# Deformable convolution, attention and routed FFN on one core: a later far list, later far sums, offset rows ahead of the projections, residual copies moved on ScalarE

## The chip, the core and the metric

The kernel runs on one core of a Trainium2 chip. The metric is the device time of one execution in microseconds. The kernel before takes 690.18 us, the median of 3 runs (689.71 to 691.6).

## The reference

The input is `x`, 4 images of 32 x 32 positions and 128 channels, all float32. Three blocks follow one another, each added to its input:

1. A deformable convolution of the group-normed `x`. A depthwise 3x3 convolution, a batch norm and SiLU give `x1`; `x1 @ off_w` gives 2-D offsets and `softmax(x1 @ mask_w)` weights, for 8 groups of channels and 9 points each. The projected input `xp` is sampled bilinearly at the 9 points (position + offset), weighted and summed, and the sum goes through `out_w`:

```
out  = corner(x0, y0, (1-fx)*(1-fy)) + corner(x0+1, y0, fx*(1-fy))
     + corner(x0, y0+1, (1-fx)*fy)   + corner(x0+1, y0+1, fx*fy)
out  = (samples * mask).sum(points) @ out_w + out_b
```

2. Attention over the 1024 tokens of each image, with layer norm ahead of it.
3. A layer norm, two routed experts of eight for each image (GELU, 128 to 256 to 128), and a layer norm of their sum.

The change touches only the first block.

## The kernel before, in words

**Sampling without a gather.** Most sample positions lie near their own place. For each position the kernel builds a 7 x 7 stencil of weights per group from "hats" (the bilinear weights of an offset against five places on each axis), and multiplies the 45 used places ("taps", the four corners of the 7 x 7 are left out) with shifted copies of `xp`. Samples whose cells fall outside the stencil are "far": they are counted, listed, fetched by GpSimd one by one with indirect DMAs, and added as a correction.

**Chunks and turns.** The work is cut into 8 chunks of 4 image rows (`CHUNKS`), with all 4 images side by side: 512 positions, 128 partitions x 4 rows. The engines run a software pipeline. In turn k:

- VectorE (`turn`, `stencils`, `products`) multiplies the taps of chunk k (L1591, 26 instructions of one or two taps) and in between prepares the stencil of chunk k+1: `mask_logits` (row_max L1447), `masks`, `weigh_hats` (L1476), `corners`, and then nine points, each an outer product (L1524) and an add into the stencil (L1532). The two kinds are interleaved by `fill`: two product instructions behind each point's outer product, `POINT_FILL`, and two more after the last add, `STENCIL_FILL`. The far list of chunk k+1 is made by `list_far(k+1)`, one MAX8 (L1578) over the counts in PSUM, ahead of the point `AT_LIST` = 4 counted from 0, the fifth. `finish_silu` (L1437) stands ahead of the sixth point. `first_stencils` prepares chunk 0 and makes list 0 at the same point. The list goes to a buffer of its own, so `list_far` waits for `far_done` (the counts are copied out) and for `list_taken` (GpSimd has copied the list before).
- TensorE (`turn` L923 on) sums each tap into a PSUM bank by four 128x128 transposes (`add_up`, L890). It waits for the product of the tap and frees its slot. There are 7 product slots, one per column of the stencil, so a tap's product can be written only when the last tap of the same column is summed. Between the sums stand, by tap number: the convolution of chunk k+2 (`AT_CONV` = 4, nine taps, L834), the counts of far samples of chunk k+1 (`AT_FAR` = 18, `count_far`, L873 to L876), the correction of chunk k-1 from GpSimd (`AT_SAMPLES` = 24, `add_fix`, L897, which waits for `fix_done`), the projection of chunk k-1, one image at every second tap (`AT_PROJECT` = 27, `project`, L909 to L912, which waits for ScalarE's `copy_out`), and the offset matmuls of chunk k+2, one row at every second tap (`AT_OFFSETS` = 32, `offsets`, L826 and L827).
- ScalarE (`turn(j)` L659, j = k) copies the offsets of chunk j+2 out (`prepare`, L590), makes its hats (L602, L608), clears the stencil (L638), makes the signs for the counts (L617) and the SiLU parts (L576, L577), copies the counts out for GpSimd (`count_out`, L647, which waits for `fix_done` of iteration j), copies the samples of chunk j out (`copy_out`, L624), and copies the projected residual of chunk j (`residual`, L632, which waits for the projection in TensorE's turn j+1).
- GpSimd runs one iteration per chunk (L1315 on): copy the list (L1322), move the places (L1323), clear and signal `list_taken` (L1326, L1327), then for each listed sample: take its offsets (L1221 to L1223), its cells (L1230 to L1240), four indirect DMAs (L1244), the corner weights (L1252 to L1277), and multiply and add what came (L1284 to L1289). At the end it signals `fix_done` (L1345).
- SyncE's queue fetches the shifted copies for the later chunks when the products of a chunk are done.

After the eighth chunk, whose products stand alone, come the attention (from about 437 us) and the FFN.

Of the kernel before, what the change touches and what calls it, by code (L numbers as in the profile page):

```python
# [40 lines left out]
CHUNKS = H // ROWS  # L41
# [21 lines left out]
UNITS = len(UNIT_AT)  # L63

BEGIN = 2
AT_CONV, AT_FAR, AT_SAMPLES, AT_PROJECT, AT_OFFSETS = 4, 18, 24, 27, 32


AT_LIST = 4


AT_SILU = 5
# [73 lines left out]
def hybrid_block_kernel(nc, x, in_w, in_b, out_w, out_b, off_w, off_b, mask_w, mask_b, dw_k, bn_g, bn_b,  # L146
                        bn_m, bn_v, attn_w, wr, br, w1, b1, w2, b2, gamma, beta, out):
    padded = nc.dram_tensor("padded", (WP, B, HP, C), F32, kind="Internal").ap()
    with ExitStack() as ctx:
# [397 lines left out]
        def _(sc):  # L547
            own = Own(sc, act)
# [62 lines left out]
            def signs_of(k):  # L611
                raw = pair[0][:, :].rearrange("p (r o) -> p r o", r=ROWS)
                if not isinstance(k, int) or k > 0:
                    sc.wait_ge(far_mm, k)
                    sc.sem_inc(act_waited, 1)
                for i, sign in enumerate((1.0, -1.0)):
                    last = sc.activation(signs[:, i, :, :], raw[:, :, 0:2 * GP], ACT.Sign,  # L617
                                         bias=tap_bias[:, TAPS - 1:TAPS], scale=sign)
                last.then_inc(signs_done, 1)
# [7 lines left out]
            def residual(k):  # L627
                sc.wait_ge(conv_out, k + 1)
                sc.sem_inc(act_waited, 1)
                to = res[:, :, :].rearrange("p (n k) c -> p n k c", n=B)[:, :, bass.ds(k, 1), :] \  # L630
                    .rearrange("p n k c -> p n (k c)")
                sc.activation(to, bank[0][:, :].rearrange("p (n c) -> p n c", n=B), ACT.Copy).then_inc(res1_done, 1)  # L632

            def clear_stencil(k):

                sc.wait_ge(prod_done, (k + 1) * NEAR)
                sc.sem_inc(act_waited, 1)
                sc.activation(stencil[:, bass.ds(k % 2, 1), :].rearrange("p s g -> p (s g)"),  # L638
                              zero_col[:, 0:1].to_broadcast([P, ROWS * G * STENCIL]), ACT.Copy
                              ).then_inc(stencil_clear, 1)  # L640
# [18 lines left out]
            def turn(j, conv_ahead):  # L659
                prepare(j + 2)  # L660
                clear_stencil(j)
                signs_of(j + 2)
                if conv_ahead:
                    silu(j + 3)
                count_out(j + 2)
                copy_out(j)
                residual(j)

            with sc.Fori(0, CHUNKS - 3) as j:
                own.enter(j, TAPS)  # L670
                turn(j, True)
                own.leave(CHUNKS - 3)
            turn(CHUNKS - 3, False)

            def residual_of(k, n0, n1):
                at = k % 2
# [702 lines left out]
        def _(ve):  # L1379
            own = Own(ve, dve)  # L1380
# [128 lines left out]
            def stencils(k, fill, silu_next):  # L1509
# [6 lines left out]
                for q in range(PTS):  # L1516
                    kx, ky = q // 3, q % 3
                    to = now[:, :, ky:ky + TAPS, kx:kx + TAPS]
                    own.wait()
                    if q == AT_LIST:  # L1520
                        list_far(k)
# [14 lines left out]
            def first_stencils():  # L1536

                ve.wait_ge(stencil_clear, 1)
                hx = hats[:, 0, :, :].rearrange("p (g q) t -> p g q t", q=PTS)
                hy = hats[:, 1, :, :].rearrange("p (g q) t -> p g q t", q=PTS)  # L1540
                full = [P, ROWS * G, TAPS, TAPS]
                size = ROWS * G * TAPS * TAPS
                spare = prod[:, :, :, :].rearrange("p s g c -> p (s g c)")
                held = [outer[:, :, :, :]] + [spare[:, i * size:(i + 1) * size].rearrange("p (g a b) -> p g a b", a=TAPS, b=TAPS)
                                              for i in range(3)]

                def place_of_point(q):
                    ky, kx = q % 3, q // 3
                    return stencil_of[:, 0, :, ky:ky + TAPS, kx:kx + TAPS]

                def point_product(q):
                    own(ve.tensor_tensor(place_of_point(0) if q == 0 else held[q % 4],
                                         hy[:, :, q, :].unsqueeze(3).to_broadcast(full),
                                         hx[:, :, q, :].unsqueeze(2).to_broadcast(full), ALU.mult))

                own.wait()
                point_product(0)
                point_product(1)
                for q in range(1, PTS):
                    if q + 1 < PTS:  # L1560
                        point_product(q + 1)
                        ve.wait_ge(dve, own.base + own.n - 1)
                    else:
                        own.wait()
                        ve.sem_inc(hats_used, 1)  # L1565
                    if q == AT_LIST:
                        list_far(0)
                    if q == AT_SILU:
                        finish_silu(1)
                    own(ve.tensor_tensor(place_of_point(q), place_of_point(q), held[q % 4], ALU.add))  # L1570
                own.wait()
# [25 lines left out]

            ve.sem_inc(res1_done, 1)
            first_stencils()
            per = own.n - n0  # L1600
            products(0, 0, BEGIN)
# [255 lines left out]
```

## Time and profile before

| | us |
|---|---|
| median of 3 runs | 690.18 (689.71 to 691.6) |
| profiled execution | 690.75 |
| its span | 688.9 |
| TensorE / VectorE / ScalarE / GpSimd busy | 588.7 / 565.8 / 234.3 / 338.8 |
| mean granted TensorE clock | 0.937 |

Busy time by stage of the profiled execution:

| stretch (us) | length | TensorE | VectorE | ScalarE | GpSimd | granted clock |
|---|---|---|---|---|---|---|
| 0 to 65.14, set-up and chunk 0's stencil | 65.14 | 52.59 | 44.81 | 30.12 | 30.24 | 0.95 |
| 65.14 to 412, turns 0 to 6 | 346.86 | 278.92 | 330.47 | 101.42 | 253.50 | 0.90 |
| 412 to 437, products of chunk 7 | 25.00 | 23.50 | 24.63 | 1.20 | 0.73 | 1.00 |
| 437 to 688.9, attention and FFN | 251.90 | 233.67 | 165.90 | 101.58 | 54.36 | 0.98 |

A busy TensorE is not TensorE at its peak, since matmuls are pipelined. The granted clock is a share of 2.4 GHz: 1.00 is 2.4 GHz and 0.50 is 1.2 GHz. Times in a timeline are microseconds from the start of the span, and a merged row is followed by the number of its instructions (x4).

### The profile page before, as it was taken

What the parts mean: (1) busy time and instruction counts of PE and PEld (TensorE: products, weight loads), DVE (VectorE), ACT (ScalarE), POOL (GpSimd) and SP (SyncE); (2) the same over time, 40 slices, a digit from 0 to 9 for tenths busy, and PEclk for the clock granted to TensorE, in tenths of its full rate; (3) what the DMA queues carried; (4) which work ended last, traced back from release to release, by engine and by line L of the source; (5) the groups of instructions that cost most, each with busy time, mean ns of one, the idle gap of its engine ahead of it and who ended that gap; (6) DMA issues with size and microseconds to landing.
All of it is one profiled execution on the core that took longest, in us unless ns stands there. A gap on an engine that the chain in (4) does not pass through costs nothing.

```text
span 688.9 us, 11121 instructions
## 1 busy us (share of the span) xinstructions
PE 588.7 (85%) x3518; PEld 434.8 (63%) x3518; DVE 565.8 (82%) x1028; ACT 234.3 (34%) x343; POOL 338.8 (49%) x407
## 2 busy tenths in 40 slices
PE   5988879879779589599786779889999999989995
PEld 4556566556556366376565567567777777775774
DVE  4589999999999699699999999726776776654877
ACT  6164306206125016107125000334545444424431
POOL 7505885888588578658667940201222221124322
PEclk9899959999999699879988799999999999999998
DMA  7096303003003007000000000000000000004111
GB/s 189 33 342 222 118 0 108 3 3 108 1 2 109 0 2 270 0 1 3 0 1 5 0 1 1 1 0 1 1 1 1 1 0 1 1 1 119 44 39 46
DMA packets 26238, 30.71 MB, mean 45 GB/s; under 512 B 5572, under 2 KB 18324, under 8 KB 26196
## 3 DMA queue, kind: packets, MB, share of 16 engines
q1 hardware_dynamic: 24094, 29.77, 13.2%
q0 software_dynamic: 1408, 0.36, 0.6%
q8 instruction: 28, 0.46, 0.3%
q10 hardware_dynamic: 694, 0.01, 0.1%
q14 instruction: 14, 0.11, 0.1%
HBM read 25.07 MB, written 5.05 MB: 44 GB/s over the span
## 4 chain that ended last, share of the span: by engine, by line
PE 38%; POOL 15%; DVE 15%; DMA 14%; issue 11%; POOLq 3%; ACT 1%; DVEq 1%; SPq 0%; ACTq 0%
DMA got<-padded,cell_now 11%; PE banks L1009 8%; PE pair L989 8%; DVE prod L1591 7%; POOL got L1244 6%; PE pair L1067 4%; PE banks L999 4%; PE banks L890 4%; PE banks L1105 4%; POOL cell_now L1240 2%; DVE stencil L1532 2%; DMA padded<-stage 2%; PE pair L834 1%; POOL place L1323 1%; POOLq L1300 1%
## 5 line engine op out<-in xcount | busy, mean ns | idle before, releaser
L890 PE MATMUL banks<-ident,prod 128*128 128x128 f32 x1440 | 219.7, 295 | 63.5 <-DVE prod L1591 61.2
L890 PEld LDWEIGHTS banks<-ident,prod 128*128 128x128 f32 x1440 | 174.2, 150 | 125.2 <-DVE prod L1591 98.4
L1591 DVE TENSOR_TENSOR prod<-shifted,stencil 128x1024 f32 (+3 forms) x208 | 216.1, 1079 | 0.1
L1349 POOL TENSOR_TENSOR rstd_now<-mv_now,neg_half 128x2 f32<-128x2 f32 x32 | 23.0, 718 | 126.1 <-DVE mv_now L1642 126.1
L834 PE MATMUL pair<-xg,dw_diag 128*128 128x512 f32 x144 | 73.4, 611 | 0.7 <-DVE xg L1403 0.7
L1244 POOL DMA_INDIRECT got<-padded,cell_now x44 | 63.6, 1446 | 19.0 <-issue 10.1
L1009 PEld LDWEIGHTS banks<-shifted 128*128 128x128 f32 x512 | 60.2, 192 | 8.1 <-issue 6.1
L1009 PE MATMUL banks<-shifted 128*128 128x128 f32 x512 | 63.3, 277 | 2.3 <-ACT shifted L714 1.4
L989 PE MATMUL pair<-shifted 128*128 128x512 f32 x128 | 60.9, 598 | 0.7 <-ACT shifted L697 0.6
L1657 DVE TENSOR_REDUCE neg_max<-pair 128x1 f32<-128x1024 f32 x32 | 39.2, 1225 | 23.0 <-PE pair L989 21.9
L1524 DVE TENSOR_TENSOR outer<-hats 128x800 f32<-128x800 f32 x56 | 56.1, 1002 | 1.2
L1532 DVE TENSOR_TENSOR stencil<-stencil,outer 128x800 f32 (+1 forms) x56 | 55.8, 997 | 0.0
L602 ACT ACTIVATE hats<-off,tap_bias 128x576 f32 (+1 forms) x40 | 48.4, 1342 | 1.3 <-DVEq L1565 0.5
L709 ACT ACTIVATE shifted<-pair,neg_max 128x1024 f32<-128x1024 f32 x32 | 35.7, 1115 | 33.5 <-DVE neg_max L1657 33.5
L1662 DVE COPY shifted<-banks 128x512 f32<-128x512 f32 x32 | 22.1, 689 | 22.5 <-PE banks L999 22.5
L1355 POOL TENSOR_TENSOR res<-res,bias_all 128x256 f32 x16 | 11.6, 727 | 46.2 <-DVE xg L1648 46.2
L999 PE MATMUL banks<-ident,shifted 128*128 128x128 f32 x256 | 34.1, 277 | 0.0
L989 PEld LDWEIGHTS pair<-shifted 128*128 128x128 f32 x128 | 22.0, 192 | 16.9 <-issue 15.3
L999 PEld LDWEIGHTS banks<-ident,shifted 128*128 128x128 f32 x256 | 30.2, 144 | 1.3 <-issue 0.2
L1067 PE MATMUL pair<-shifted,stage 128*128 128x512 f32 x64 | 29.3, 597 | 1.5 <-DMA stage<-in_L_ffn_W_dram 1.5
L632 ACT ACTIVATE res<-banks 128x512 f32 (+1 forms) x6 | 3.6, 597 | 79.0 <-PE banks L912 79.0
L834 PEld LDWEIGHTS pair<-xg,dw_diag 128*128 128x128 f32 x144 | 23.9, 197 | 10.0 <-issue 10.0
(250 smaller groups left out, 918.8 us busy)
## 6 DMA issues: line engine op xcount, KB each, us to landing
shifted<-padded SPq DMA_DIRECT2D x42, 256.0 KB
shifted<-padded SPq DMA_DIRECT2D x14, 640.0 KB
res<-in_x_dram SPq DMA_DIRECT2D x4, 512.0 KB, 6.2
padded<-stage SPq DMA_DIRECT2D x4, 512.0 KB, 11.8
stage<-in_L_ffn_W_dram SPq DMA_DIRECT2D x16, 128.0 KB, 2.1
out_dram<-res SPq DMA_DIRECT2D x16, 128.0 KB, 1.8
got<-padded,cell_now POOLq DMA_INDIRECT x44
padded<-stencil SPq DMA_DIRECT2D x2, 228.0 KB, 2.6
```

The lines of the kernel that those rows point to most:

```text
L602: own(sc.activation(hats[:, :, :, t].rearrange("p a (r g) -> p a r g", r=ROWS), off[:, bass.ds(k % OFFS, 1), :, 0:2 * GP].rearrange("p s r ...
L834: mm = pe.matmul(conv_bank.rearrange("c (r a) -> c r a", r=ROWS), dw_diag[:, t, :], src, start=(t == 0), stop=(t == 8))
L890: mm = pe.matmul(acc_of(c, r), prod[:, slot, r * G:(r + 1) * G, :].rearrange("p g c -> p (g c)"), ident[:, :], is_transpose=True, start=(t ...
L989: mm = pe.matmul(pair[s][:, h * 512:(h + 1) * 512], keyed[:, bass.ds(i * P, P)], normed_t[:, bass.ds((i // TILES) * TOK + h * 512, 512)], ...
L999: mm = pe.transpose(bank[h][:, m * P:(m + 1) * P], probs[:, s, (4 * h + m) * P:(4 * h + m + 1) * P], ident[:, :])
L1009: mm = pe.matmul(bank[2][:, 0:C], probs_t[:, m * P:(m + 1) * P], normed[:, bass.ds((i // TILES) * TILES + m, 1), :].rearrange("p t c -> p ...
L1067: pe.matmul(pair[j][:, (f % 2) * 512:(f % 2 + 1) * 512], w1_sel[:, 2 * (q // 2) + j, (f % 2) * P:(f % 2 + 1) * P], normed2_t[:, q * 512:(q ...
L1244: gp.indirect_dma_start(out=got[:, j, a, :], out_offset=None, in_=table, in_offset=bass.IndirectOffsetOnAxis(ap=cell_now[:, j, a:a + 1], a ...
L1524: own(ve.tensor_tensor(to if q == 0 else outer[:, :, :, :], hy[:, :, q, :].unsqueeze(3).to_broadcast(full), hx[:, :, q, :].unsqueeze(2).to ...
L1532: own(ve.tensor_tensor(to, to, outer[:, :, :, :], ALU.add))
L1591: ins = ve.tensor_tensor(prod[:, dx:dx + n, :, :], shifted[:, dx:dx + n, bass.ds(((c % HALF) * ROWS + dy) * G, ROWS * G), :], stencil_of[: ...
L1657: ve.tensor_reduce(neg_max[:, s:s + 1], pair[s][:, :], AX.X, ALU.max, negate=True).then_inc(max_done, 1)
```

## The change

Five edits. The far list of chunks 1 to 7 is made ahead of the ninth stencil point, `AT_LIST` = 8; that of chunk 0 stays at the fifth, under the name `FIRST_LIST`. On TensorE the correction (`add_fix`) goes from tap 24 to tap 31, also in the last chunk, where `AT_SAMPLES` is used by itself. The projections go from taps 27, 29, 31, 33 to taps 35, 37, 39, 41. The offset rows go from taps 32, 34, 36, 38 to taps 30, 32, 34, 36, so that they stand ahead of the projections. On ScalarE `residual(j - 1)` stands behind `prepare(j + 2)` and `clear_stencil(j)`, where `residual(j)` stood at the end of the turn; turn 0, which has none, is written out ahead of the loop, and the last one follows turn 5.

```diff
-AT_CONV, AT_FAR, AT_SAMPLES, AT_PROJECT, AT_OFFSETS = 4, 18, 24, 27, 32
+AT_CONV, AT_FAR, AT_OFFSETS, AT_SAMPLES, AT_PROJECT = 4, 18, 30, 31, 35
...
-AT_LIST = 4
+FIRST_LIST, AT_LIST = 4, 8
...
             def turn(j, conv_ahead):
                 prepare(j + 2)
                 clear_stencil(j)
+                if not isinstance(j, int) or j > 0:
+                    residual(j - 1)
                 signs_of(j + 2)
                 if conv_ahead:
                     silu(j + 3)
                 count_out(j + 2)
                 copy_out(j)
-                residual(j)
-
-            with sc.Fori(0, CHUNKS - 3) as j:
+
+            turn(0, True)
+            with sc.Fori(0, CHUNKS - 4) as j:
                 own.enter(j, TAPS)
-                turn(j, True)
-                own.leave(CHUNKS - 3)
+                turn(j + 1, True)
+                own.leave(CHUNKS - 4)
             turn(CHUNKS - 3, False)
+            residual(CHUNKS - 3)
...
-                    if q == AT_LIST:
+                    if q == FIRST_LIST:
                         list_far(0)
```

## Rows read from the trace of the kernel before

**Rows 1.** Busy time per stretch: turns 1 and 3; length, busy by engine, granted clock, DMA

```profile
112.98:160.57 47.59, 39.73 (x242) 28.46 (x241) 46.86 (x54) 16.05 (x17) 39.56 (x37) 0.96 0.15 43
...
208.76:262.35 53.59, 41.87 (x242) 29.62 (x241) 47.07 (x55) 15.72 (x16) 38.89 (x47) 0.87 0.12 35
```

**Rows 2.** Waits of VectorE, 0 to 445 us: total us, times, longest

```profile
DVE far_list L1578 <- POOLq L1326: 11.9, 2, 6.0
```

**Rows 3.** Timeline, VectorE, turns 1, 3 and 4: start, us, engine, line, operation

```profile
151.32 0.99 DVE L1532 TENSOR_TENSOR stencil<-stencil,outer 128x800 f32 x1
...
156.50 4.15 DVE L1591 TENSOR_TENSOR prod<-shifted,stencil 128x1024 f32 x4
...
237.93 0.45 DVE L1578 MAX8 far_list<-pair 1x8 f32<-1x288 f32 x1 [5.94 <-POOLq L1326]
...
291.53 0.45 DVE L1578 MAX8 far_list<-pair 1x8 f32<-1x288 f32 x1 [5.96 <-POOLq L1326]
```

**Rows 4.** Timeline, GpSimd, iterations 1 to 7: list copies and last samples

```profile
105.65 1.17 POOL L1322 CAST far_list_i<-far_list 1x8 int32<-1x8 f32 x1 [2.48 <-issue]
...
174.35 0.80 POOL L1284 TENSOR_TENSOR got<-got,w_now 128x64 f32<-128x64 f32 x1 [0.44 <-DMA got<-padded,cell_now]
...
177.51 0.22 POOL L1289 TENSOR_TENSOR stage<-stage,got_sum 128x16 f32 x1 [0.42 <-POOL got_sum L1287]
...
179.64 0.18 POOL L1322 CAST far_list_i<-far_list 1x8 int32<-1x8 f32 x1 [1.90 <-ACT far_counts L647]
...
232.51 0.29 POOL L1284 TENSOR_TENSOR got<-got,w_now 128x64 f32<-128x64 f32 x1 [0.45 <-DMA got<-padded,cell_now]
...
233.85 0.22 POOL L1289 TENSOR_TENSOR stage<-stage,got_sum 128x16 f32 x1 [0.42 <-POOL got_sum L1287]
...
236.14 0.18 POOL L1322 CAST far_list_i<-far_list 1x8 int32<-1x8 f32 x1 [2.06 <-ACT far_counts L647]
...
289.73 0.18 POOL L1322 CAST far_list_i<-far_list 1x8 int32<-1x8 f32 x1 [2.07 <-ACT far_counts L647]
...
340.09 3.40 POOL L1322 CAST far_list_i<-far_list 1x8 int32<-1x8 f32 x1 [4.92 <-DVE far_list L1578]
...
404.21 0.99 POOL L1322 CAST far_list_i<-far_list 1x8 int32<-1x8 f32 x1 [2.06 <-issue]
```

**Rows 5.** Timeline, VectorE, beside the list copy at 340.09

```profile
342.47 0.97 DVE L1532 TENSOR_TENSOR stencil<-stencil,outer 128x800 f32 x1
```

**Rows 6.** Timeline, TensorE, turns 0, 1 and 4 and the last correction

```profile
98.81 1.11 PE L890 MATMUL banks<-ident,prod 128*128 128x128 f32 x4 [0.89 <-DVE prod L1591]
...
148.30 0.39 PE L909 MATMUL banks<-out_w_sb,xg 128*128 128x128 f32 x2
...
149.09 0.60 PE L890 MATMUL banks<-ident,prod 128*128 128x128 f32 x4
149.53 0.53 PE L826 MATMUL pair<-offmask_w,gate 128*128 128x216 f32 x2
...
150.19 1.32 PE L890 MATMUL banks<-ident,prod 128*128 128x128 f32 x8
...
288.96 1.12 PE L897 MATMUL banks<-ident,stage 128*128 128x128 f32 x4 [3.60 <-POOLq L1345]
...
299.55 0.64 PE L909 MATMUL banks<-out_w_sb,xg 128*128 128x128 f32 x2
...
300.92 1.73 PE L890 MATMUL banks<-ident,prod 128*128 128x128 f32 x8
...
435.77 0.60 PE L897 MATMUL banks<-ident,stage 128*128 128x128 f32 x4
```

**Rows 7.** Busy time per stretch in turn 0, columns as in the first group

```profile
100.00:104.00 4.00, 4.00 (x15) 2.58 (x15) 3.97 (x5) 0.00 (x0) 2.57 (x4) 0.50 0.00 0
104.00:108.00 4.00, 4.00 (x29) 3.26 (x29) 3.96 (x5) 0.36 (x1) 2.26 (x2) 0.96 0.01 2
```

**Rows 8.** The page's costliest groups: ScalarE's residual copy

```profile
L632 ACT ACTIVATE res<-banks 128x512 f32 (+1 forms) x6 | 3.6, 597 | 79.0 <-PE banks L912 79.0
```

## Prediction

> **What bounds the kernel now.** I read the busy time per stretch first [rows 1]. A stretch there is one turn of the convolution loop, from one row_max of VectorE to the next. From 112.98 to 160.57 us (turn 1) VectorE is busy for 46.86 of 47.59 us: a turn is a VectorE pass. Turn 3 (208.76 to 262.35) takes 53.59 with the same VectorE work. The list of waits, cut to VectorE, names the difference [rows 2]: the MAX8 that makes the far list (L1578) waits for GpSimd's L1326 twice, 11.9 us in total. The timeline puts the waits ahead of the MAX8s at 237.93 (turn 3) and 291.53 (turn 4) [rows 3]. 11.9 us is all that this change can win.
>
> Why they wait: a new list may be written only when GpSimd has copied the last one (list_taken), the first thing in each of its iterations. Iterations 2, 3 and 4 begin with the copies at 179.64, 236.14 and 289.73 [rows 4], 56.5 and 53.6 us apart against VectorE's 47.6. VectorE arrives 5.9 us early in turn 3, is set back, and again in turn 4. Iteration 4 has no far sample, after which the queue is empty.
>
> **List at the ninth point.** In turn 1 the eighth point's add ends at 152.31 (151.32 + 0.99) [rows 3]; with the MAX8 behind it, less the MAX8's own 0.4 further up, the new MAX8 would start at 151.9, 38.9 us into the turn. Turn 3 reaches it at 208.76 + 38.9 = 247.7, and the list is free at 237.9: that wait is gone, 5.94 us. Turn 4 begins 5.94 earlier, at 256.4, and reaches it at 295.4; with GpSimd as it was (free at 291.5) that wait would be gone too. Behind the MAX8 on VectorE stand the last point's product and four tap products; for it wait GpSimd's next iteration and, a turn later, the count matmuls. In turn 0 (65.14 to 112.98) it would end about 104.6; iteration 1, which needs it, starts at 105.65: no cost.
>
> **But GpSimd will not be as it was.** Its short instructions end when VectorE's do. The copy at 340.09 takes 3.40 us, to 343.49; VectorE's running add ends at 343.44, the fourth instruction since its MAX8. While VectorE stands still the same copy takes 0.18, at 236.14 and at 289.73 [rows 4, 5]. The last sample of an iteration, from multiply to add, takes from 232.51 to 234.07 (1.56 us) while VectorE waits, but from 174.35 to 177.73 (3.38) while it works. The waits that the change removes sped GpSimd up. Iteration 2 loses 1.8 of that and iteration 3 begins about 238.0. Iteration 3, two samples, then lies wholly beside a busy VectorE. The other two-sample iterations bound its length: iteration 2 with a slow last sample, 56.5 + 1.8 = 58.3; iteration 6, busy throughout, 404.21 - 340.09 = 64.1. I take the middle, 61.2, since it starts in another phase of the turn than either. Iteration 4 then begins at 296.3, 298.7 or 300.3 (by the middle and the high value its last sample falls partly or wholly in VectorE's new wait, 0.5 and 1.8 back). The MAX8 comes 1.8 after that copy (291.53 against 289.73): 298.1, 300.5 or 302.1, against an arrival at 295.4. The wait in turn 4 is 2.7, **5.1** or 6.7 us.
>
> The Trainium skill, SBUF — State Buffer, section "SBUF: two separate sides", states that a VectorE instruction with two SBUF inputs and a GpSimd instruction that reads SBUF exclude each other, and that the loser goes on when the winner ends. Taken as one VectorE instruction at most per GpSimd instruction, it would cut the 3.40 to some 1.2, iteration 6 to 61.9, the middle to 60.1 and the wait to about 4.3. The copy's row outlasts several instructions, so I keep the rows.
>
> **Far sums at tap 31.** TensorE's add of the corrections (L897) waits for fix_done of the same iteration. In turn 4 it is wanted at tap 31, about 289, and released 0.8 before the next copy (288.96 against 289.73): near 298. Everything behind it on TensorE waits: tap sums 31 on, three offset rows, four projections. VectorE is held only through its seven product slots: it can finish tap 37, and needs tap 32 summed for tap 39. Prices [rows 6]: at full clock a tap 0.44 (149.09 to 149.53), an offset row 0.66, a projection 0.79 (148.30 to 149.09); at the low one a tap 0.87 (1.73 for two taps), a projection 1.37, an offset row by the same ratio 1.15. The correction is four transposes like a tap. From the release to the sum of tap 41 that is 19.4 us low, 10.4 full. VectorE needs tap 41 for the second pair of the next chunk's products, at 159.4 in turn 1 (two and a half products into the run at 156.50), 7.5 after the MAX8, and the MAX8 comes 2.6 after the release: 10.1. After such a stall the granted clock is 0.50; in turn 0 it came back near 104.3 [rows 7], 5.5 us after TensorE ran without a gap from 98.81. With 5.5 us low, tap 41 comes at 12.9: VectorE loses **2.8**. Bounds: full clock at once 0.3, low throughout 9.3.
>
> **Offsets ahead of the projections.** TensorE's work is the same, packed into taps 30 to 41 in every turn where it was 24 to 38. Without a stall it is 11.5 us at full clock and 21.4 at the low one; from tap 30 ready (142.9) to the need of tap 41 (159.4) are 16.5. Taps 19 to 30 now hold nothing but tap sums, as in turn 0, where the clock was 0.50 until past 104. With 5.5 us low they take 14.0: margin 2.5, cost 0; low throughout would cost 4.9 a turn. The offsets themselves end about 2 us earlier, but the row_max that reads them waited for nothing (it directly follows the products of 156.50): no gain. After the late release of turn 4 they end near 308, ahead of the next row_max at 304.1 + 7.9 = 312: covered.
>
> **Residual copies behind the hats.** They are 0.60 us each [rows 8], no longer ahead of the hats and now ahead of the signs. What needs the signs is TensorE's count at tap 18, behind nine convolution taps, and VectorE needs the count first at its MAX8. Cost 0, at most 0.6 a turn if the count were held up with the tap sums behind it. Without the move the hats would wait for the projections of tap 41. GpSimd's last iterations start up to 12 us later, since list 6 comes near 351.8 where it came at 339.5: iteration 7 begins near 416 (404.21 before) and takes some 6. The last correction, at 435.77 before and 431.8 then, finds it done: cost 0.
>
> **Sum.** 11.9 - 5.1 - 2.8 = 4.0 us. The profiled execution took 690.75 us (span 688.9), which makes 686.75; it lies 0.57 above the median of the runs, 690.18, so the median becomes **686.2**.
>
> **Rivals.**
> (A) The forecast: one wait stays in turn 4, and TensorE catches up behind it. From 2.7 + 0.3 to 6.7 + 9.3 lost, most of it 682 to 689. Chance 0.50.
> (B) GpSimd keeps its pace and both waits go: 690.2 - 11.9 = 678.3, up to 681. It decides if iteration 4 begins by 293.6, a slip of under 3.9 us. For it: iteration 3 needed only 53.6, and begun at 238.0 that would do. Against it: 3.38 against 1.56 for the last sample, and iteration 6's 64.1. Chance 0.20.
> (C) The wait moves whole: a long iteration 3 and a low clock give back 10 to 14 us, 688.3 to 692. Moving the list wins nothing, since GpSimd's chain sets the pace up to iteration 4. Chance 0.19.
> (D) Slower: the dense taps 30 to 41 starve the product slots in every turn, because the clock is still low there. It decides when the clock comes back more than 10 us into the stretch; up to 4.9 us in each of turns 1 to 5. At 2.5 us it is 12.5 against 4.0 won: 698.7. Against it is turn 0, with the same gap ahead of its offsets and no VectorE wait. Chance 0.11.
>
> **Numbers.** 0.3% is 2.1 us, about what a measurement of this kernel can tell from no change. Faster: B 0.20, of A 0.44, of C 0.03, so 0.67. Same: A 0.04, C 0.13, D 0.03, so 0.20. Slower: A 0.02, C 0.03, D 0.08, so 0.13. The range, 678.4 to 690.8, runs from the full gain to the middle of C; it leaves out D and the end of C, 0.15.
>
> **What would show it.** Turn 3 at 47.6 us with no wait at L1578. In turn 4 a wait at L1578 for L1326 of 3 to 7 us, the copy that begins iteration 4 at 296 or later, last samples of iteration 2 at 3.4 us, TensorE idle at L897 for up to 9 us, and then VectorE waiting at L1591 for TensorE, which it does nowhere now. No wait at L1578 at all is B; waits at L1591 in turns 1 and 2 are D. I am wrong if turn 3 still waits or if another line holds VectorE.

## The result, and the profile after

The changed kernel takes **708.86 us** (median of 4 runs, 702.43 to 712.08), against 690.89 (689.71 to 691.69, 4 runs) for the kernel before on the same chip. The ratio is 1.025 [1.0165, 1.0335]: slower, by more than the noise (whether by more than 2%, the interval leaves open), where 686.2 was predicted, and outside the range. The profiled execution took 711.73 us (span 709.9, mean granted clock 0.90). Behind ScalarE's `turn` (L659) lines stand 3 further down than before, ahead of it where they were: the MAX8 is L1581, the products L1594, the tap sums L893, the correction L900, GpSimd's list copy L1325, its `fix_done` L1348, row_max L1450.

The page of the kernel after, its busy times and three of its costliest groups:

```profile
PE 596.8 (84%) x3518; PEld 449.0 (63%) x3518; DVE 566.7 (80%) x1028; ACT 233.4 (33%) x343; POOL 371.6 (52%) x407
...
L1594 DVE TENSOR_TENSOR prod<-shifted,stencil 128x1024 f32 (+3 forms) x208 | 217.1, 1078 | 20.6 <-PE banks L893 20.3
...
L900 PE MATMUL banks<-ident,stage 128*128 128x128 f32 x32 | 8.2, 409 | 34.1 <-POOLq L1348 34.1
...
L1325 POOL CAST far_list_i<-far_list 1x8 int32<-1x8 f32 x8 | 18.1, 2259 | 27.6 <-DVE far_list L1581 11.2
```

VectorE is as busy as before (566.7 against 565.8). GpSimd is busy 32.8 us longer (371.6 against 338.8) with the same instructions, and two waits have grown: the products, which waited for no tap sum before, wait 20.3 us for them, and TensorE's correction waits 34.1 us for GpSimd's `fix_done`, against 6.7 before.

VectorE's waits of the kernel after, 0 to 470 us (total, times, longest), which answer to [rows 2]:

```profile
DVE prod L1594 <- PE banks L893: 20.3, 16, 12.1
DVE far_list L1581 <- POOLq L1329: 10.8, 3, 4.6
```

31.1 us in place of 11.9, 19.2 more. That is all but 1.8 of the 21.0 by which the spans differ (709.9 against 688.9). The list wait did not go away: 11.9 us in two waits became 10.8 in three, and the slot waits came on top.

Busy time per stretch of the kernel after, turns 1 to 4 (row_max to row_max) and the products of chunk 7, columns as in [rows 1]:

```profile
112.07:159.59 47.52, 42.35 (x242) 31.32 (x241) 46.76 (x54) 15.13 (x15) 37.37 (x27) 0.86 0.14 41
159.59:211.72 52.13, 42.58 (x236) 31.16 (x236) 47.81 (x54) 15.57 (x16) 38.80 (x45) 0.80 0.14 46
211.72:266.77 55.05, 40.29 (x244) 30.28 (x242) 47.78 (x54) 15.58 (x16) 40.57 (x47) 0.84 0.13 36
266.77:323.19 56.42, 41.77 (x244) 31.24 (x242) 47.79 (x54) 15.56 (x16) 39.03 (x44) 0.82 0.18 69
...
418.00:456.00 38.00, 24.63 (x182) 21.78 (x181) 24.87 (x32) 0.60 (x1) 26.16 (x26) 0.82 0.00 1
```

Turn 1 is as short as ever. Turns 2, 3 and 4 are 4.5 to 8.8 us too long, and the last chunk's products, 25 us before, take 12 more. So something made GpSimd late in turn 1, and again ahead of the last chunk. The timeline of the kernel after names it. GpSimd, iterations 1 to 7: each copy of a list, and every instruction of over 3 us beside them:

```profile
104.24 7.95 POOL L1325 CAST far_list_i<-far_list 1x8 int32<-1x8 f32 x1 [4.39 <-ACT off L590]
112.27 4.54 POOL L1326 TENSOR_SCALAR place<-place 128x288 f32<-128x288 f32 x1
...
151.82 8.11 POOL L1243 TENSOR_SCALAR cell_now<-cell_f,cell_at 128x4 uint32<-128x4 f32 x1
160.69 3.48 POOL L1247 DMA_INDIRECT got<-padded,cell_now  x1 [0.77 <-POOL cell_now L1243]
...
198.40 0.70 POOL L1325 CAST far_list_i<-far_list 1x8 int32<-1x8 f32 x1 [1.92 <-ACT far_counts L647]
...
253.88 0.18 POOL L1325 CAST far_list_i<-far_list 1x8 int32<-1x8 f32 x1 [2.06 <-ACT far_counts L647]
...
308.94 0.18 POOL L1325 CAST far_list_i<-far_list 1x8 int32<-1x8 f32 x1 [2.07 <-ACT far_counts L647]
...
313.66 0.18 POOL L1325 CAST far_list_i<-far_list 1x8 int32<-1x8 f32 x1 [3.25 <-issue]
...
363.12 7.95 POOL L1325 CAST far_list_i<-far_list 1x8 int32<-1x8 f32 x1 [11.24 <-DVE far_list L1581]
371.15 4.54 POOL L1326 TENSOR_SCALAR place<-place 128x288 f32<-128x288 f32 x1
...
409.93 27.46 POOL L1255 TENSOR_TENSOR tap_d<-low,got_here 128x16 f32<-128x16 f32 x1
...
447.28 0.18 POOL L1325 CAST far_list_i<-far_list 1x8 int32<-1x8 f32 x1 [2.06 <-issue]
```

A copy of eight numbers takes 7.95 us, and a subtraction on 16 columns 27.46 us. VectorE beside the first and the last of them, same kernel:

```profile
103.61 0.45 DVE L1581 MAX8 far_list<-pair 1x8 f32<-1x288 f32 x1 [0.17 <-DVE stencil L1535]
104.00 0.96 DVE L1527 TENSOR_TENSOR outer<-hats 128x800 f32<-128x800 f32 x1
104.89 2.34 DVE L1594 TENSOR_TENSOR prod<-shifted,stencil 128x1024 f32<-128x1024 f32 x2
107.16 0.97 DVE L1535 TENSOR_TENSOR stencil<-stencil,outer 128x800 f32<-128x800 f32 x1
108.06 4.08 DVE L1594 TENSOR_TENSOR prod<-shifted,stencil 128x1024 f32<-128x1024 f32 x4
112.07 0.43 DVE L1450 TENSOR_REDUCE row_max<-off 128x32 f32 x1
...
115.67 0.43 DVE L1465 TENSOR_REDUCE row_sum<-mask 128x32 f32<-128x288 f32 x1
...
409.27 0.45 DVE L1581 MAX8 far_list<-pair 1x8 f32<-1x288 f32 x1 [0.18 <-DVE stencil L1535]
...
413.71 23.59 DVE L1594 TENSOR_TENSOR prod<-shifted,stencil 128x1024 f32<-128x1024 f32 x24
449.44 1.23 DVE L1594 TENSOR_TENSOR prod<-shifted,stencil 128x1024 f32<-128x1024 f32 x1 [12.14 <-PE banks L893]
```

The copy starts 0.2 us after the MAX8 ends and itself ends at 112.19, just after the eight two-input instructions that follow the MAX8 without a gap, when row_max (one input) has begun. The subtraction ends at 437.39, VectorE's run at 437.30 (413.71 + 23.59), when VectorE stands still for want of a slot. GpSimd got in nowhere in these two stretches, at none of the ends of some 28 VectorE instructions in the second. The first did not end for good at row_max either: the next GpSimd row, L1326 at 112.27, took 4.54 us and ended at 116.81, 1.14 after row_sum began (before, the same instruction behind its copy at 105.65 took 2.08).

The rest follows. Iteration 1 takes 94.2 us (104.24 to 198.40) where it took 74.0 [rows 4], and iterations 2 and 3 take 55.5 and 55.1, longer than a turn of VectorE (47.6). So VectorE waits for the list in turns 2 to 4 (1.65, 4.57 and 4.58 us at their MAX8s) and for slots behind the late corrections (2.1, 2.2 and 3.8 us). Iteration 6 takes 84.2 (64.1 before): TensorE's correction in the last chunk waits until 446.51, and the products 12.14 us.

### The profile page after: what moved, and what is told of

It is laid out like the page before. It is cut to its first block, busy times and chain, and to the rows that moved or that the text cites. A ratio compares the mean times of both kernels' runs of the same rounds, so it can differ in the third digit from the quotient of the medians.

```text
span 709.9 us, 11109 instructions
## 1 busy us (share of the span) xinstructions
PE 596.8 (84%) x3518; PEld 449.0 (63%) x3518; DVE 566.7 (80%) x1028; ACT 233.4 (33%) x343; POOL 371.6 (52%) x407
## 4 chain that ended last, share of the span: by engine, by line
PE 42%; POOL 19%; DMA 15%; DVE 10%; issue 8%; POOLq 3%; ACT 2%; DVEq 0%; SPq 0%; ACTq 0%
DMA got<-padded,cell_now 14%; PE banks L1012 8%; PE pair L992 8%; POOL got L1247 6%; PE banks L893 5%; PE pair L1070 4%; PE banks L1002 4%; PE banks L1108 4%; POOL cell_now L1243 3%; DVE prod L1594 3%; PE pair L837 2%; POOL far_list_i L1325 2%; POOL place L1326 2%; PE pair L829 1%; DVE stencil L1535 1%
## 5 line engine op out<-in xcount | busy, mean ns | idle before, releaser
L893 PE MATMUL banks<-ident,prod 128*128 128x128 f32 x1440 | 223.3, 305 | 49.4 <-DVE prod L1594 48.5
L893 PEld LDWEIGHTS banks<-ident,prod 128*128 128x128 f32 x1440 | 185.6, 157 | 102.1 <-DVE prod L1594 72.6
L1594 DVE TENSOR_TENSOR prod<-shifted,stencil 128x1024 f32 (+3 forms) x208 | 217.1, 1078 | 20.6 <-PE banks L893 20.3
L1247 POOL DMA_INDIRECT got<-padded,cell_now x44 | 62.0, 1410 | 19.0 <-issue 10.1
L992 PE MATMUL pair<-shifted 128*128 128x512 f32 x128 | 62.4, 611 | 0.7 <-ACT shifted L700 0.6
L602 ACT ACTIVATE hats<-off,tap_bias 128x576 f32<-128x576 f32 (+1 forms) x40 | 48.4, 1339 | 1.7 <-DVEq L1534 0.9
L900 PE MATMUL banks<-ident,stage 128*128 128x128 f32 x32 | 8.2, 409 | 34.1 <-POOLq L1348 34.1
L647 ACT ACTIVATE far_counts<-pair 1x288 int32<-1x288 f32 (+1 forms) x8 | 3.2, 397 | 95.1 <-POOLq L1348 78.4
L624 ACT ACTIVATE xg<-banks 128x512 f32<-128x512 f32 (+1 forms) x8 | 4.8, 597 | 89.3 <-PE banks L900 89.3
L1002 PE MATMUL banks<-ident,shifted 128*128 128x128 f32 x256 | 34.1, 277 | 0.0
L1325 POOL CAST far_list_i<-far_list 1x8 int32<-1x8 f32 x8 | 18.1, 2259 | 27.6 <-DVE far_list L1581 11.2
```

What stands on the lines that cost most here:

```text
L602: own(sc.activation(hats[:, :, :, t].rearrange("p a (r g) -> p a r g", r=ROWS), off[:, bass.ds(k % OFFS, 1), :, 0:2 * GP].rearrange("p s r ...
L893: mm = pe.matmul(acc_of(c, r), prod[:, slot, r * G:(r + 1) * G, :].rearrange("p g c -> p (g c)"), ident[:, :], is_transpose=True, start=(t ...
L992: mm = pe.matmul(pair[s][:, h * 512:(h + 1) * 512], keyed[:, bass.ds(i * P, P)], normed_t[:, bass.ds((i // TILES) * TOK + h * 512, 512)], ...
L1002: mm = pe.transpose(bank[h][:, m * P:(m + 1) * P], probs[:, s, (4 * h + m) * P:(4 * h + m + 1) * P], ident[:, :])
L1247: gp.indirect_dma_start(out=got[:, j, a, :], out_offset=None, in_=table, in_offset=bass.IndirectOffsetOnAxis(ap=cell_now[:, j, a:a + 1], a ...
L1594: ins = ve.tensor_tensor(prod[:, dx:dx + n, :, :], shifted[:, dx:dx + n, bass.ds(((c % HALF) * ROWS + dy) * G, ROWS * G), :], stencil_of[: ...
```

## The experiments

Medians are of 4 runs where nothing else is said. Each ratio is to runs of the kernel before on the same chip (its medians lay between 691.44 and 691.73); medians of two variants may come from different chips.

**One part alone: the list, or the order.** e1 is the kernel before with the later list only; e2 is the changed kernel with all but the later list. (e1 also calls list 0 by `FIRST_LIST`, as the change does.)

```diff
-AT_LIST = 4                 (e1, from before)
+FIRST_LIST, AT_LIST = 4, 8
-FIRST_LIST, AT_LIST = 4, 8  (e2, from after)
+FIRST_LIST, AT_LIST = 4, 4
```

> Only the far list is moved to the ninth stencil point (chunks 1 to 7); TensorE's and ScalarE's order stay as in the kernel before. Theory S (GpSimd starves while VectorE runs without a pause, and the later list starts its iterations at the head of such a run): the list copies of iterations 1 and 6 take some 8 us, iteration 1 over 85 us, VectorE waits again in turns 2 to 4 and in the last chunk, 698 to 712 us. Theory O (the loss is from the new order on TensorE): no loss here, 680 to 691 us.

> The whole change but the far list, which stays at the fifth point. S: GpSimd's iterations are as in the kernel before, so 688 to 694 us, with two list waits of about 6 us. O: the order costs in every turn and most of the loss stays, 700 to 710 us, with VectorE waiting for product slots.

Measured: e1 724.94 us, ratio 1.0481 [1.0458, 1.0504]; e2 691.14 (10 runs), 0.9999 [0.9981, 1.0018]. The whole loss is the list's, and with the list at the fifth point the order of TensorE and the residual copies cost nothing. Alone the list is even worse than with the order, and beyond the 698 to 712 that I expected: VectorE waits 44.3 us for slots, against 20.3 in the changed kernel. That TensorE's correction at tap 24 stands ahead of more taps than at tap 31 fits this, and e1 waits 14.71 us for it once. e1, timeline of TensorE and, below it, of GpSimd in the last chunk:

```profile
312.08 1.11 PE L897 MATMUL banks<-ident,stage 128*128 128x128 f32 x4 [14.71 <-POOLq L1345]
...
419.69 23.14 POOL L1244 DMA_INDIRECT got<-padded,cell_now  x1 [0.30 <-issue]
```

Here the row kept out for 23 us was an indirect DMA's issue, not a subtraction: it is not a matter of one operation.

**Pauses in VectorE.** e3 lets VectorE wait for its own products after every fourth product instruction of the last chunk (five waits); e4 does the same, and in every turn also ahead of and behind the first products of the next chunk.

```diff
-            products(CHUNKS - 1, BEGIN, UNITS)
+            for u in range(BEGIN, UNITS, 4):
+                end = min(u + 4, UNITS)
+                products(CHUNKS - 1, u, end)
+                if end < UNITS:
+                    ve.wait_ge(prod_done, (CHUNKS - 1) * NEAR + UNIT_AT[end][0])
...
+                    ve.wait_ge(prod_done, (k + 1) * NEAR)                       (e4)
                     fill(BEGIN)
+                    ve.wait_ge(prod_done, (k + 1) * NEAR + UNIT_AT[BEGIN][0])   (e4)
```

> The changed kernel, with VectorE in the last chunk waiting for its own products after every fourth product instruction (5 pauses). S: each pause lets one GpSimd instruction in, the instruction of 27 us beside the last chunk falls to under 6 us, and most of the wait of 12 us for the correction of chunk 6 goes: 5 to 12 us less than the changed kernel. Rival (GpSimd is late by its DMAs or by its start alone): the wait of 12 us stays, 0 to 2 us more than the changed kernel.

> As the run before, and in every turn VectorE also waits for its own products once before and once after the first products of the next chunk (14 more pauses, about 0.2 us each by the 0.17 us that the MAX8 waits for the add before it). S: the list copies and the instructions at that place fall from 8 us to under 5, iteration 1 ends some 5 to 8 us earlier, the list waits of turns 2 to 4 shrink, 680 to 696 us. Rival (the length of iteration 1 is not from the run without pauses): its length stays near 94 us and the pauses only cost 3 us.

Measured: e3 704.15, 1.0167 [1.0138, 1.0195]; e4 695.49 (5 runs), 1.0065 [1.0038, 1.0093]. In e4 the list copy of iteration 1 takes 5.67 us and the iteration 78.2. The theory had the blocked rows too short (under 6 us in e3, under 5 in e4). e3, timeline of GpSimd in the last chunk:

```profile
411.40 11.96 POOL L1255 TENSOR_TENSOR tap_d<-low,got_here 128x16 f32<-128x16 f32 x1
423.32 0.73 POOL L1257 TENSOR_TENSOR cell_at<-pos,low 128x8 f32<-128x8 f32 x1
424.13 1.10 POOL L1258 TENSOR_TENSOR tap_c<-side,tap_d 128x32 f32<-128x32 f32 x1
425.21 1.17 POOL L1262 TENSOR_SCALAR frac<-cell_at 128x8 f32<-128x8 f32 x1
```

The blocked instruction ends 11.96 us in, not 27.46, VectorE's wait for the correction falls from 12.14 to 7.3 us, and after that row GpSimd mostly gets one instruction in for each one of VectorE (about 1.1 us), with only the few pauses of the edit between them. So a pause does not have to be there each time. There are two kinds of run of VectorE: in one GpSimd gets its turn at nearly every seam (the end of one VectorE instruction and the start of the next), in the other it gets none for many seams, until VectorE next pauses. I then looked where the second kind begins. In the six profiles so far, that of before too, 41 GpSimd rows between 60 and 480 us are longer than 3 us. 29 of them had started within 1.4 us of a MAX8; the other 12 stand right behind such a row, at row_max, like L1326 above, and "nearly every" in g1's expectation passes over them. The copy at 340.09 (3.40 us) [rows 4], 0.2 after the end of the MAX8 of 339.46, is one of the 29. Timeline of VectorE in the kernel before:

```profile
339.46 0.45 DVE L1578 MAX8 far_list<-pair 1x8 f32<-1x288 f32 x1 [0.17 <-DVE stencil L1532]
...
343.57 0.69 DVE L1437 SCALAR_TENSOR_TENSOR gate<-gate,conv 128x512 f32<-128x512 f32 x1
```

The MAX8 at the fifth point is followed by a pause of VectorE after its fourth instruction, as `finish_silu` waits for the add (343.44 to 343.57). The one at the ninth point has none before row_max, and in the last chunk none before VectorE runs out of slots.

**A pause right behind the MAX8.** One line, in `list_far`:

```diff
             ve.max(far_list[:, :], pair[1][0:1, 0:FAR_COLS]).then_inc(listed, 1)
+            ve.wait_ge(listed, k + 1)
```

g1 is the changed kernel with it, g2 the kernel before with it, g3 is e1 with it, h3 is e2 with it, and g4 is g1 with the list at the seventh point (`AT_LIST` = 6).

> The changed kernel, with VectorE waiting for its MAX8 to end before it goes on (a pause of 0.1 to 0.2 us, 7 times). In all six profiles so far nearly every GpSimd instruction of over 3 us began within 1.4 us of a MAX8, and beside the last chunk's products of the run with pauses GpSimd got in at every seam once one pause had come. Theory M (after a MAX8 with no pause behind it VectorE's chain keeps GpSimd out until its next pause): the instructions of 8 and 27 us are gone, none over 4 us near a MAX8, iteration 1 falls from 94 to 70 to 80 us, and the time to 678 to 692 us. Theory S (any run without a pause keeps it out): the run behind the ninth point is still 8 us, and the time stays at 700 to 712 us.

> The kernel before, with the same wait behind the MAX8. M: the instructions of 3.4 to 3.9 us at 88, 137, 340 and 387 us fall to about 1.2; iterations 1 and 6 shorten by 2 to 4 us, the two list waits of 6 us shrink a little, 686 to 691 us. S: the segment behind the fifth point has pauses anyway, nothing changes, 690 to 693 us.

> Only the list at the ninth point, TensorE and ScalarE as in the kernel before, and the wait behind the MAX8. M: the loss of 33 us of the list alone mostly goes, but TensorE now meets the correction at tap 24 before GpSimd has it, so VectorE waits for product slots in turns 3 and 4: 686 to 700 us, and slower than the changed kernel with the same wait. S: near 725 us as without the wait.

> The changed kernel with the wait behind the MAX8 and the list ahead of the seventh point. M: no long GpSimd instruction, list ready 8 us earlier than at the ninth, 678 to 690 us, within 4 us of the run at the ninth point. S: the run behind the seventh point is 4 us long at most, so it beats the ninth point by over 8 us, lock or no lock.

> The new order on TensorE and ScalarE, the list at the fifth point, the pause behind the MAX8: the last corner of the table of list place, order and pause. M: as the kernel before with the pause, since neither correction nor offsets bound it: 686 to 691 us, with waits for list_taken of 4 to 6 us in turns 3 and 4. Rival (the order is what wins once the lock is gone): 680 to 684 us.

| list of chunks 1 to 7 | order | without the pause | with it | ratio with it |
|---|---|---|---|---|
| fifth point | before | 691.56 | 689.06 (g2, 7 runs) | 0.9944 [0.992, 0.9967] |
| fifth | after | 691.14 (e2) | 689.07 (h3, 10 runs) | 0.9958 [0.9938, 0.9978] |
| seventh | after | not run | 682.08 (g4) | 0.9841 [0.9798, 0.9883] |
| ninth | before | 724.94 (e1) | 686.25 (g3) | 0.9903 [0.9868, 0.9938] |
| ninth | after | 708.86 | **681.74** (g1) | 0.9849 [0.9818, 0.988] |

One wait behind the MAX8, eight times, is worth 27 us in the changed kernel, 39 in e1 and 2.5 in the kernel before. The pause is 0.04 us long, and the outer product starts 0.1 us later after the start of the MAX8 than without it (0.49 against 0.39). **g1 beats both kernels.** g1, timeline of VectorE and GpSimd in turn 0, and busy time of turns 3 and 4:

```profile
104.77 0.45 DVE L1581 MAX8 far_list<-pair 1x8 f32<-1x288 f32 x1 [0.17 <-DVE stencil L1535]
105.26 0.99 DVE L1527 TENSOR_TENSOR outer<-hats 128x800 f32<-128x800 f32 x1
106.17 2.58 DVE L1595 TENSOR_TENSOR prod<-shifted,stencil 128x1024 f32<-128x1024 f32 x2
...
105.40 0.90 POOL L1325 CAST far_list_i<-far_list 1x8 int32<-1x8 f32 x1 [7.59 <-DVE far_list L1581]
106.38 2.07 POOL L1326 TENSOR_SCALAR place<-place 128x288 f32<-128x288 f32 x1
```

```profile
209.37:257.35 47.98, 39.48 (x242) 28.59 (x241) 47.27 (x54) 15.56 (x16) 35.20 (x41) 0.93 0.13 38
257.35:305.75 48.40, 39.69 (x242) 28.43 (x241) 47.60 (x54) 15.59 (x16) 33.42 (x35) 0.93 0.24 93
```

The copy takes 0.90 in place of 7.95, iteration 1 takes 72.3, iteration 6 58.1, and VectorE waits for no list and 0.5 us in all for slots. The two kinds of run also differ on VectorE's side: after the MAX8 without a pause the outer product and the pair of products take 0.96 and 2.34, with it 0.99 and 2.58. VectorE loses a little time to GpSimd where it lets it in, and none where it doesn't.

With the list at the ninth point and the pause, the order of TensorE comes to matter: in g3 the correction at tap 24 waits 8.85 us for GpSimd in turn 4 and holds the slots once, 4.87 us at 291.76, which g1 at tap 31 has not. The medians, 686.25 and 681.74, differ by 4.5. The two intervals overlap a little, but all four runs of g1 (up to 682.07) lie under all four of g3 (from 684.22) on the same chip. With the list at the fifth point the order is worth nothing (g2 689.06, h3 689.07).

**Is it the place, or any pause?** h1 puts a wait of VectorE for all its own work behind the outer product of the seventh point, ahead of the MAX8; h2 behind that of the ninth, one instruction after it. Neither has one directly behind the MAX8.

```diff
+                    if q == AT_LIST - 2:    (h1; h2: if q == AT_LIST:)
+                        own.wait()
                     fill(POINT_FILL[q])
```

> Control: the changed kernel with a pause of the same kind at another place, behind the seventh point's outer product, and none behind the MAX8. M: the chain behind the MAX8 is as long as before, the list copies still take some 8 us and the time stays at 700 to 713 us. Rival (the gain of the pause behind the MAX8 is from a small shift in time, or from any extra pause in the turn): 680 to 695 us.

> The changed kernel with the pause one instruction later, behind the ninth point's outer product, none right behind the MAX8. M: what begins in the outer product waits for its end only (under 2 us), so nearly the whole gain: 679 to 688 us. Rival (it must be the MAX8 itself that VectorE waits for): the copies still take 8 us, 700 to 713 us.

Measured: h1 702.13 (5 runs), 1.0159 [1.0127, 1.0191], with copies of 7.94 us and L1255 at 27.45 again (its profiled run was its slowest, 714.65); h2 684.41, 0.9907 [0.9888, 0.9926], copy 0.76, iteration 1 72.6. A pause ahead of the MAX8 does nothing for GpSimd; one after it, right behind or one instruction on, cures it. So the MAX8 begins the blocked run, and a pause behind it ends it, at each place where one was tried. A pause that nobody put in does the same: in the last chunk of k2 below, VectorE waits 0.30 us for a slot at 415.86, and the GpSimd row blocked since 408.80 ends at 415.99.

**What is it in the MAX8?** It reads PSUM, is a MAX8, and works on one partition. i1, k1 and k2 are g1 with one more instruction between the pause and the outer product. Its result is not used, and `own(...)` adds no wait (`own.link(...)` does); j1 and j2 keep the MAX8 but change what stands last ahead of the outer product, with no pause behind it.

```diff
+            own(ve.tensor_reduce(rden[:, 0:1], tap_bias[:, :], AX.X, ALU.max))                                (i1, 128 x 6)
+            own(ve.tensor_reduce(rden[:, 0:1], mask[:, :, :].rearrange("p g q -> p (g q)"), AX.X, ALU.max))   (k1, 128 x 288)
+            own(ve.tensor_reduce(rden[0:1, 0:1], tap_bias[0:1, :], AX.X, ALU.max))                            (k2, 1 x 6)
...
+            own.link(ve.tensor_copy(far_sb, pair[1][0:1, 0:FAR_COLS]))                                        (j1)
+            ve.max(far_list[:, :], far_sb).then_inc(listed, 1)
...
+            own.link(ve.max(far_list[:, :], pair[1][0:1, 0:FAR_COLS]))                                        (j2)
+            ve.tensor_reduce(far_one[:, :], pair[1][0:1, 0:FAR_COLS], AX.X, ALU.max).then_inc(listed, 1)
```

> What arms the lock-out: the changed kernel with the pause behind the MAX8, and behind that pause, ahead of the outer product and with no pause of its own, one more instruction of another kind that has a single input: a maximum over six columns in SBUF on 128 partitions (it adds nothing to the output). If any such instruction in front of the chain arms it, the copies that begin iterations 1 and 6 take some 8 us again and the time is 698 to 712 us. If it must be the MAX8 (or its input in PSUM, or its one partition), the time is that of the run with the pause plus about 1.5 us for the added instructions, 680 to 686 us.

> The changed kernel, where the counts are first copied from PSUM to SBUF, VectorE waits for the copy, and the MAX8 reads the copy in SBUF, with no pause behind it. If the MAX8 itself arms the lock-out: the copies that begin iterations 1 and 6 take some 8 us again, 700 to 713 us. If the PSUM input does: they take about 1 us, 682 to 688 us (the copy and its pause cost about 0.6 us a turn).

> The changed kernel with a pause behind the MAX8, and behind the pause a plain maximum over the same 288 counts in PSUM on one partition, with no pause behind it; GpSimd starts at its end. If the PSUM input on one partition arms the lock-out: copies of 8 us, 700 to 713 us. If the MAX8 does: about 1 us, 682 to 688 us.

> The changed kernel with the pause behind the MAX8, then a maximum over 288 columns of SBUF on 128 partitions (0.45 us, it adds nothing to the output) and no pause behind it. If the length of the single-input instruction arms the lock-out (VectorE then has the next instructions lined up behind it): GpSimd instructions of 8 us and more behind the ninth point, 700 to 716 us. If its one partition does: none over 3 us there, 683 to 688 us.

> The same with a maximum over six columns of SBUF on one partition (0.16 us). If the length arms the lock-out: none over 3 us there, 680 to 686 us. If the one partition does: instructions of 8 us, 700 to 716 us.

| last ahead of the chain, no pause behind it | us | ratio | first list copy |
|---|---|---|---|
| MAX8, 1 partition, PSUM (the change) | 708.86 | 1.025 [1.0165, 1.0335] | 7.95 |
| j1: MAX8, 1 partition, SBUF | 714.35 | 1.0323 [1.0291, 1.0355] | 7.95 |
| j2: reduce, 1 partition x 288, PSUM | 709.83 | 1.028 [1.023, 1.033] | 13.05 |
| k2: reduce, 1 partition x 6, SBUF | 701.97 | 1.0166 [1.0111, 1.0222] | 8.14 |
| i1: reduce, 128 partitions x 6, SBUF | 682.55 | 0.9867 [0.9835, 0.9898] | 0.96 |
| k1: reduce, 128 partitions x 288, SBUF | 684.4 | 0.9895 [0.9863, 0.9927] | 0.18 |

k2 and i1 are the pair that counts: the same operation on six columns behind the same pause. k2, timeline of VectorE and GpSimd, and the same of i1 under it:

```profile
104.61 0.15 DVE L1583 TENSOR_REDUCE rden<-tap_bias 1x1 f32<-1x6 f32 x1
104.69 0.97 DVE L1527 TENSOR_TENSOR outer<-hats 128x800 f32<-128x800 f32 x1
...
112.77 0.43 DVE L1450 TENSOR_REDUCE row_max<-off 128x32 f32 x1
...
104.76 8.14 POOL L1325 CAST far_list_i<-far_list 1x8 int32<-1x8 f32 x1 [4.39 <-ACT off L590]
```

```profile
105.54 0.16 DVE L1583 TENSOR_REDUCE rden<-tap_bias 128x1 f32<-128x6 f32 x1
105.62 0.98 DVE L1527 TENSOR_TENSOR outer<-hats 128x800 f32<-128x800 f32 x1
...
105.69 0.96 POOL L1325 CAST far_list_i<-far_list 1x8 int32<-1x8 f32 x1 [4.40 <-ACT off L590]
```

In both the reduce takes 0.15 or 0.16, the outer product starts 0.08 after its start, and GpSimd's copy 0.07 after that. On one partition the copy takes 8.14 us and ends at row_max (112.90); on 128 it takes 0.96. k1's copy (0.18) ran beside the reduce itself, ahead of the chain; the row behind it, L1326, took 2.01 us, as in g1 (2.07). Neither the operation nor PSUM nor the length decides, but the single partition; only 1 and 128 were tried. The whole traces agree. In the eight runs with a pause behind the MAX8 (or one instruction on) and no one-partition instruction behind it, g1 to g4, h2, h3, i1 and k1, no GpSimd row from 60 to 480 us is longer than 3.01 us; in the kernel before, the changed one and the eight other runs the longest are 3.93 to 28.05.

j2's 13.05 is a longer row of the same kind. Timeline of GpSimd and VectorE:

```profile
106.27 13.05 POOL L1326 CAST far_list_i<-far_list 1x8 int32<-1x8 f32 x1 [8.07 <-DVE far_one L1583]
...
114.10 0.43 DVE L1451 TENSOR_REDUCE row_max<-off 128x32 f32 x1
...
119.19 0.33 DVE L1469 RECIPROCAL row_sum<-row_sum 128x32 f32<-128x32 f32 x1
```

It outlasts row_max and, at 117.70, row_sum, and ends at 119.32. So a one-input instruction on 128 partitions does not always let GpSimd in.

## Why the prediction was wrong

**What bounds the kernel: right.** The two list waits were the one thing to win, and with the pause they were won: g1 is 9.8 us under the kernel before (691.56 to 681.74), where the waits were 11.9. 2.5 of the 9.8 the pause gives without the change (g2).

**"Iteration 1 ... starts at 105.65: no cost": this step failed.** The list was there in time (the MAX8 ended at 104.06), as predicted. In the terms of the sum, the list waits cost 10.8 us where 5.1 stood, and the slot waits 20.3 where 2.8 stood. What I did not price was the instruction that takes the list over. It now starts with VectorE's MAX8 just done and a run without a pause ahead, and took 7.95 in place of 1.17; its neighbour (4.54) and L1243 one turn later (8.11) were kept out as well, and iteration 1 became 20.2 us longer. The pattern lay in my own rows: I read in [rows 4, 5] that the copy at 340.09 ended with "the fourth instruction since its MAX8", and used it only as a price of 1.8 us per iteration, not as "until VectorE next pauses". Moving the MAX8 moved it away from the pause behind the fifth point, and the question what pause comes after the ninth was never asked.

**"The last correction ... finds it done: cost 0": failed for the same reason.** List 6 was 23 us later than before (363.12 against 340.09), about 12 of it predicted. That alone would still have been covered: with the 64.1 of before, iteration 6 ends near 427 (363.12 + 64.1), ahead of the 434 at which TensorE came to the correction (446.51 - 12.24). The 27.46 us of L1255 were not; VectorE waited 12.1.

**Iterations 2 and 3, "58.3 to 64.1", middle 61.2: too high.** They took 55.5 and 55.1 in the changed kernel, where VectorE still waited, and 57.2 and 57.1 in g1, where it did not. The slow last sample was real; that iteration 3 should go beyond iteration 2's own slow pace was not. So iteration 4 began at 291.95 in g1, under the 293.6 that I gave as rival B's condition, and g1's turn 4 has no list wait. With the pause in place what happens is nearly B: 681.74, just above its 678.3 to 681. But GpSimd did not keep its pace unaided, as B had it; the pause gave it back, so this does not make B right.

**TensorE's catching up, 2.8 us in one turn: near in size, wrong in number.** Turn 4 lost 3.8 us to slots, in waits of at most 1.4. But turns 2 and 3 lost 2.1 and 2.2 too, as their corrections were late as well, and the last chunk 12.1.

**Order on TensorE and residual copies, cost 0: right.** e2 says 0.9999 [0.9981, 1.0018], with the list at the fifth point. Turn 1 of the changed kernel, 47.52 us at a granted clock of 0.86 without a slot wait, refutes rival D. The rival on the slower side was looked for on TensorE; it sat on GpSimd.

**The Trainium skill's rule.** The case's traces go beyond it. A GpSimd instruction stays out across eight and some 28 VectorE instructions with two SBUF inputs. The Trainium skill, SBUF — State Buffer, section "A bandwidth-pool intuition that's wrong (but worth ruling out)", has a GpSimd-issued DMA blocked beside a VectorE copy go on about 115 ns after the end of VectorE's instruction. By the one-at-a-time reading of the lock I would have had 4.3 in place of 5.1 for the wait in turn 4; that reading fits e3's row after row of about 1.1 us, and not the 7.95 and 27.46. I kept the rows over it, rightly, but took from them only a size.

**What stays open.** Why one partition matters is not settled, nor what lies between 1 and 128. Nor is it settled what a one-input seam on 128 partitions does to a blocked run: in the changed kernel three rows ended at row_max (the copies of iterations 1 and 6, and L1243), but the row after each was kept out again until about row_sum; in j1 and j2 four rows lasted past both. A GpSimd row can also span up to three VectorE seams with no MAX8 near: in g1 some take 2.7 to 3.0 us. The list at the seventh point without the pause was not run. g1 is not told apart from g4, i1 and k1 (681.74 to 684.4) by their intervals; that of h2 (684.41) begins just above g1's.

## What to carry to other kernels

When an instruction is moved on one engine, look at what another engine starts on its signal, and at when the first engine pauses next: a long GpSimd row that ends where VectorE pauses is a price that grows with the distance to that pause. If VectorE does something on a single partition (a MAX8, a scalar-like reduce) and then a chain of two-input SBUF instructions, try a wait for that instruction's own result; here each such wait cost 0.1 us at its place, and with it the change brought 1.5% where alone it lost 2.5%. And when a good change loses, try it again with the disturbance taken out before dropping it: with the pause the list at the ninth point wins (686.25 alone, 681.74 with the order), and at the seventh as much (682.08).

## What the runs showed of the hardware

- Behind a one-partition VectorE instruction with no pause, VectorE's two-input SBUF instructions kept GpSimd out altogether: 7.95 us over 8 of them, 27.46 over some 28, and an indirect DMA's issue for 23.14. The same reduce on 128 partitions did not do this (8.14 against 0.96 us).
- In a chain of the other kind GpSimd mostly got in once per VectorE instruction (1.10 and 1.17 us in e3) and waited for three seams at most (up to 3.01 us in k1), and the chain paid for it (2.58 against 2.34 us for two products).
- VectorE waiting for its own last result, a pause of some 0.04 us, was enough to change the one kind into the other.
